# Second attention of a fused four-layer kernel: own work of VectorE, ScalarE and GpSimd put on other steps, and each step's new scores ahead of its shifted scores

## The reference

```python
qkv = x @ Wqkv + bqkv                      # 16 heads of 8 numbers, 512 tokens a sequence
q = _apply_rope(q, cos, sin); k = _apply_rope(k, cos, sin)
scores = jnp.einsum('bhqd,bhkd->bhqk', q, k) * scale
attn = jax.nn.softmax(scores, axis=-1)
out = jnp.einsum('bhqk,bhkd->bhqd', attn, v)
return out.transpose(0, 2, 1, 3).reshape(b, s, dim) @ Wout + bout
```

## Time and profile before

| | us |
|---|---|
| median of three runs | 2768.68 (2757.35 to 2777.84) |
| profiled execution | 2750.51 |
| its span in the trace | 2748.7 |
| of it the second attention, from its first normalised rows to its last power | about 949, from 1609 to 2558 |

### The profile page before, as it was taken

The page is one execution under the profiler, slowest core; times in us unless marked ns, Lnnn a source line. Parts: engine busy times, 40 slices in busy tenths (PEclk is TensorE's granted clock), DMA queues, the critical chain, the costliest instruction groups (busy, mean ns, idle before and its releaser), DMA issues. The chain is left out here.

```text
span 2748.7 us, 73587 instructions
## 1 busy us (share of the span) xinstructions
PE 2061.8 (75%) x26748; PEld 1195.5 (43%) x26748; DVE 1992.3 (72%) x5289; ACT 1552.3 (56%) x2872; POOL 1218.4 (44%) x1067
## 2 busy tenths in 40 slices
PE   5988989888988896411009928888888888888587
PEld 3776767676767675400004402232222322322354
DVE  4676767676777666688407817898888988987698
ACT  5665656565655563100004416787777777877587
POOL 5666666666667562000263357632432343230122
PEclk9999999999999998555559968999999999999799
DMA  4333333333333331000022232221112212220001
GB/s 115 75 79 72 71 77 74 75 80 72 79 76 75 71 73 25 1 0 0 19 64 76 81 70 49 51 41 27 25 32 34 33 26 31 35 32 2 13 23 35
DMA packets 103680, 136.73 MB, mean 50 GB/s; under 512 B 23781, under 2 KB 78981, under 8 KB 103046
## 3 DMA queue, kind: packets, MB, share of 16 engines
q1 hardware_dynamic: 99206, 123.34, 20.7%
q0 software_dynamic: 4096, 8.40, 1.1%
HBM read 26.52 MB, written 12.58 MB: 14 GB/s over the span
## 5 line engine op out<-in xcount | busy, mean ns | idle before, releaser
L1788 DVE TENSOR_REDUCE d_nmax_<-d_s_ 128x2 bf16<-128x1024 f32 x512 | 614.9, 1222 | 128.6 <-PE d_s_ L1950 126.9
L1699 ACT ACTIVATE d_pT_<-d_t_ 128x512 f32<-128x512 f32 x1024 | 558.2, 601 | 170.8 <-PE d_t_ L1962 163.3
L268 POOL TENSOR_TENSOR a_other<-a_other,a_rope 128x512 f32<-128x512 f32 x256 | 323.2, 1284 | 358.0 <-DMA a_other<-a_raw 357.2
L1975 PE MATMUL d_o_<-d_pT_,d_v_ 128*32 128x256 f32 x4096 | 326.3, 403 | 0.2 <-ACT d_pT_ L1699 0.2
L1962 PE MATMUL d_t_<-d_qs_,d_ks_ 49*128 49x512 bf16 x1024 | 207.7, 402 | 86.8 <-ACT d_pT_ L1699 41.6
L336 ACT ACTIVATE a_pT<-a_t 64x384 f32<-64x384 f32 x512 | 248.3, 485 | 19.2 <-PE a_t L588 7.5
L476 DVE RECIPROCAL a_rden<-a_o 128x512 f32<-128x512 f32 x64 | 214.7, 3355 | 49.5 <-PE a_o L601 49.4
L299 ACT COPY a_v<-a_proj 128x512 f32<-128x512 f32 x128 | 74.9, 585 | 278.8 <-PE a_proj L499 278.8
L460 DVE TENSOR_REDUCE a_nmax<-a_s 128x4 bf16<-128x384 f32 x256 | 130.7, 552 | 134.7 <-PE a_s L565 134.3
L1950 PE MATMUL d_s_<-d_ks_,d_qs_ 48*128 48x512 bf16 x1024 | 206.9, 400 | 17.5 <-DVE d_nmax_ L1788 12.1
L1155 ACT ACTIVATE c_hT_<-c_in_,c_beta_,c_gamma_ 128x512 f32<-128x512 f32 x16 | 12.4, 777 | 328.0 <-PE c_in_ L1275 328.0
(11 more groups left out here) (260 smaller groups left out, 4641.6 us busy)
## 6 DMA issues: line engine op xcount, KB each, us to landing
a_other<-a_raw SPq DMA_DIRECT2D x512, 128.0 KB, 2.3
d_qs_<-d_part_ SPq DMA_DIRECT2D x192, 64.0 KB
d_ks_<-d_part_ SPq DMA_DIRECT2D x192, 64.0 KB
a_xpre<-x SPq DMA_DIRECT2D x16, 256.0 KB, 3.8
a_xres<-x SPq DMA_DIRECT2D x16, 256.0 KB, 3.5
c_xs_<-sorted_x SPq DMA_DIRECT2D x16, 256.0 KB, 2.7
c_w_<-e_w SPq DMA_DIRECT2D x16, 256.0 KB, 3.3
sorted_x<-c_xs_ SPq DMA_DIRECT2D x16, 256.0 KB, 2.0
```

The lines of the kernel that those rows point to most:

```text
L268: nc.gpsimd.tensor_tensor(other[s % 2][:, side, :], other[s % 2][:, side, :], rope[:, 1, :], ALU.mult).then_inc(rope2_done, 1)
L1699: nc.scalar.activation(pT[kt][pair][:, a, :], t_bank(j, turn)[:], ACT.Exp).then_inc(t_read, 1)
L1788: nc.vector.reduce_max(out, s_bank(unit, e)[:], AX_X, negate=True).then_inc(s_read, 1)
L1975: ins = nc.tensor.matmul(o_ps[HC * i:HC * (i + 1), cols], v[e.k][:, kt, g * GH + i, :], pT[kt][i // 2][:, i % 2, cols], start=(kt, half) = ...
```

## The change

The tables are rewritten: most of a block's own work moves to later steps, and work of PE, ACT and DVE is put on the same steps where possible. `STACK`, `SHIFTS`, `VALUES` and `AHEAD` stay. In PE's step `scores` now comes ahead of `shifted`.

```diff
-    LAST = 74
-
-    STAT_IN, STAT_IN2, ROOT_IN, NORM_IN, NORM_IN2 = -56, -55, -53, -50, -49
-    FOR_ACT = {"turn_in": -46, "q0": -45, "q1": -44, "q2": -43, "q3": -42, "v": -28, "att": 41, "y": 44}
+    LAST = 92
+
+    STAT_IN, STAT_IN2, ROOT_IN, NORM_IN, NORM_IN2 = -60, -55, -52, -47, -45
+    FOR_ACT = {"turn_in": -42, "q0": -41, "q1": -40, "q2": -39, "q3": -37, "v": -28, "att": 41, "y": 44}
-    ROPE = (-44, -43, -42, -41)
-    FIRST_PART, SECOND_PART = (-40, -37), (-36, -35)
-    REST, THIRD_PART = (-39, -37), (-35, -34)
+    ROPE = (-40, -39, -38, -36)
+    FIRST_PART, SECOND_PART = (-36, -33), (-34, -31)
+    REST, THIRD_PART = (-35, -33), (-32, -31)
-    STAT_Y, STAT_Y2, ROOT_Y, NORM_Y, NORM_Y2, ADD_Y = 48, 49, 51, 56, 59, 63
-    STAT_SUM, STAT_SUM2, ROOT_SUM = 67, 68, 74
+    STAT_Y, STAT_Y2, ROOT_Y, NORM_Y, NORM_Y2, ADD_Y = 55, 56, 57, 62, 63, 64
+    STAT_SUM, STAT_SUM2, ROOT_SUM = 86, 91, 92
...
             def step(turn, n):
-                e = of(turn, n, n)
-                if e is not None:
-                    shifted(e, n)
                 unit = unit_at(n)
                 e = of(turn, n, unit - AHEAD)
                 if e is not None:
                     scores(e, unit)
+                e = of(turn, n, n)
+                if e is not None:
+                    shifted(e, n)
```

## The result

The changed kernel took **2784.7 us** in the median of 20 runs (2762.8 to 2796.5), the kernel before 2767.6 on the same chip (20 runs): ratio 1.0050, 95% interval [1.0032, 1.0067]: 14 us more by the ratio, 17 between the medians. That is within 1%, on the other side of the 5 us less that were forecast. The profiled execution took 2788.05 us. The 2750.51 of the profile before lay 17 us under its kernel's median on this chip and under all 20 of these runs, and on which chip it was taken is not on record. So the two traces can't be subtracted without a second look at before; the experiments give it.

What follows compares the result with a forecast made beforehand. No engine fills the second attention: a DMA gate at step 16, couplings in the second half and the jump back bound it. Terms -1 - 9 + 4 + 1 = -5 us give 2764 from 2768.7; range 2732 to 2790.

Steps and rivals of the forecast that it cites:

- The gate: PE's stop at step 16, set by the queue of DMAs: the first half does not move, worth 0.
- The side bet: PE's stop at step 16 for `nmaxT` grows from 2.57 to about 4 us in odd blocks.
- The jump back: Where the loop jumps back: DVE, behind PE, works during PE's stop; 1.8 us gained five times, 9 us.
- The second half: Halves from step 16 without a jump: net gain 0.1 us each, 1 us over 10 block boundaries.
- The normalised output: Moved to steps 30 and 31, its pieces run into POOL's `rest`: 0.5 us more, bounds 0 and 1.8.
- Rival B: At DVE's steps 30 and 31 both output pairs meet POOL, delaying the gate: +27, 2796 us; chance 0.15.
- The slow clock: PE idles longer ahead of step 16; three more blocks get the slow clock at 1.2 us: 4 us lost.
- Ends: Run-in and run-out: block 1's projections move beside maxima, 1 us lost; block 0's gathers 0, between 0 and 3.
- Rival A: Second half runs at DVE's pace, nothing collides, and the jump's 2.9 us vanish: 2734 us; chance 0.25.
- C: Nothing moves: the gate and PE's stop hide gain and loss, 2769 us; chance 0.60 together with the forecast.

Runs made afterwards that it cites:

- e2: Kernel before with the new tables alone, old order kept: 2795.9 us, ratio 1.0062 to before.
- e14: Kernel before with the new tables in the old order, gathers paced one per step: 2765.5 us, ratio 1.0050 to before.
- e16: Kernel before with new tables and new order, gathers paced one per step: 2755.6 us, ratio 1.0010 to before.
- e6: Changed kernel with DVE's statistics of y and of the sum moved off POOL's rotation: 2750.9 us, ratio 0.9987 to before.
- e8: Changed kernel with DVE's statistics moved off POOL's rotation and the gathers paced: 2747.9 us, ratio 0.9986 to before.
- e15: Kernel before with the old tables in the new order, gathers paced: 2735.4 us, ratio 0.9936 to before.
- e13: Kernel before with its 48 gathers paced one per step, nothing else changed: 2753.5 us, ratio 0.9999 to before.
- e7: Changed kernel with POOL issuing no gather ahead of ACT, one per step: 2760.0 us, ratio 1.0037 to before.
- e10: Changed kernel run again unchanged, gathers unpaced: 2788.4 us, ratio 1.0046 to before.
- e9: Kernel before run again unchanged, its third profile: 2769.4 us.
- e4: Changed kernel without the 48 row gathers of blocks 0 and 1 and the wait for them: 2756.1 us.

## Why the prediction was wrong

**The gate (first half, worth 0): right.** First halves averaged 25.8 to 27.3 us in every kernel but those with tables alone, and the chain from transpose to PE stayed at 21.4 to 21.9. The side bet failed: PE's stop did not grow to 4 us. Over 14 gates it averages 1.9, 1.7 and 1.5 us in three profiles of before, 1.3, 1.1, 1.35 and 0.9 in four of the changed kernel; in the odd blocks of the forecast 2.4 to 2.7 became 1.9 to 2.4. The relieved DVE waits for PE instead at steps 5 and 13 (1.2 to 1.9 and 0.5 us a block in four profiles of the changed kernel, 0.6 to 0.8 and 0 in four of before).

**The jump back (-9): the step that failed.** I had DVE behind PE through steps 28 to 31, so that it would work during PE's stop. It does, with the new tables in the old order: 0.03 to 0.08 us of gap (`e2`, `e14`), and the halves with a jump take 29.9 to 30.1 us, 1.4 to 1.7 less than the kernel before, near the 1.8 that I had taken. But the change also swaps the order, which I had counted at the gate, and elsewhere only for ACT: DVE is given each unit earlier in every step and has caught up by the jump. On steps 30 and 31 its maximum starts 1.7 and 1.2 us behind `shifted` in `e14`, 0.2 and 0.8 in `e16`. Its gap is 2.2 to 2.8 us, PE's stop 3.2 to 3.7 on average in place of 3.0 to 3.2, and the halves with a jump take 30.9 to 32.0 us, before 30.6 to 31.9. Gain 0, where 9 us were forecast. I also took block 9's 29.32 us as typical; the five such halves of that profile average 30.6.

**The second half (-1): sign wrong.** Without a jump (blocks 4 to 12, even) it takes 27.2 us in every profile of the changed kernel, 26.55 to 26.96 in four of before: +0.3 to +0.7 for each edge. The term missing is the meeting of DVE's small operations with POOL's rotation: its 1.37 us on step 29 are more than this difference, and 27.2 less 1.4 is an estimate of 25.8 us without it. No kernel that ran shows that half, since `e6` and `e8` load other steps instead. The order's own part was right: I had taken 1.13 us off, and `e15` is 1.3 under `e13` there. I had followed POOL to steps 29 to 1, where `rest` and `third part` moved, and not to 24 to 28, where I knew that `ROPE` moved (the table of steps under the change has it), and had priced the aggregation by clean records. It costs DVE about 1.85 us in a block (`ROOT_Y` up to 934 for 170 ns, `mean` 1261 for 170), 23 us in a profile, where the collision of the normalised output had cost 13.8 before. Moving the work away gave 12 us of the kernel (`e8` against `e7`).

The Trainium skill (SBUF — State Buffer, "Who interferes with whom") says that of a VectorE operation in a two-port mode and one of GpSimd the first to issue gets the shared pair of ports for the whole instruction, and that issue order decides who blocks, not the shape. The trace agrees: POOL's product issued at 2190.10, DVE's copy at 2190.13, and their records end together at 2191.4. I had applied the rule to the pieces that had collided before, when it asks for every eligible operation of DVE against every tile of POOL.

**The normalised output (+0.5 a block in it): did not happen**, 352 ns at most, since the new order lets DVE finish before `rest` begins. Rival B needs the old order: with it, 2.40 us for a pair and 29.6 us first halves, as its mechanism said.

**The slow clock (+4): of the right order, in another place.** The loop spends 48 to 72 us at the lower clock in four profiles of the changed kernel, 38 to 58 in four of before (one of them paced); the ranges overlap. I had put the added part behind a longer stop at the gate, which did not come: stretches that begin around step 16 sum to 14 to 27 us, before 17 to 31. Those at the jumps make it, with 24 to 51 us where before had 21 to 27. That the size was near is luck.

**Ends (+1, gathers 0 within 0 to 3): the size was off.** On a chip with late starts, as the profile of the measurement shows them (147.0 us), it is +12.3 us (`e10` against `e9`). I had looked whether ACT has slack for a later second part, not what POOL does once released. The first profile could not show it: it came from a quiet execution or a quiet chip.

The sum as measured: blocks 0 and 1 +12.3. The loop, with second halves, jump and clock in it, +2.6: it averages 669.7 us in nine profiles with the new tables and order (664.9 to 674.5; gathers as they are, paced or left out) and 667.1 in four of the kernel before (664.6 to 668.8). That makes +15, where the ratio says +14 and the medians +17; the +12.3 rest on one profile of each kernel. On a quiet chip, with pacing, it is +2. **Rival A** was not seen: the second half takes 25.6 us at best (`e15`, 24.1 of them PE's), and that with the old tables. **Rivals B and C** lie about as far from the result in number (+27 and 0), and neither's mechanism made it. That the time lies inside the range that I gave is luck too: 12 of the 15 us came from blocks 0 and 1, which I had put at 1 us and their gathers at 0.

## What to carry to other kernels

When work moves in time, list every operation of VectorE that can meet GpSimd against every long tile of GpSimd at the new places, not only the pair that met before; here a copy of four numbers waited as long as the tile of 512 beside it took. And look at what the new place holds: in halves without a jump the move of `e6` saved 1.37 us on one step and cost 1.2 on others. A queue that runs ahead of its consumers and is then held by one wait releases a burst: where bursts hurt, pace it by the work beside it. Split a change into its parts: here the swap of two calls alone, with the gathers paced, beats both kernels (0.9875 and 0.9936 of before, 34.7 and 17.6 us by the ratios), and the tables cost up to 20 us.

## What the chip showed that I had not expected

Matmuls were recorded as done and their readers started up to 11 us later, often on two engines at once and with no engine of the kernel named as releaser, only where GpSimd issued row gathers (none in `e4`), and on some chips only: 42 to 65 us of such waits in unpaced kernels on P and R, 0.2 at most on Q. On S every profiled kernel was paced and showed none, and pacing the kernel before left its time there at 0.9999. Spaced to one a step they came to 19 and 9 us on R. Whether a signal, the record of the matmul or something else is late these traces do not show.
